# Weights in pieces, first loads in the order of use, last store by tiles: an RNN, LSTM, transformer block and expert layer in one kernel

## The reference

```python
x = x + rnn(x, cond)            # h = tanh(x_t Wx + b + h Wh), over 512 tokens
x = x + lstm(x, cond)           # four gates of 256, over 512 tokens
x = x + block(x, cond)          # hyperbolic attention (16 heads) and MLP, modulated by cond @ w_ada + b_ada
x = x + experts(x, cond)        # a shared MLP and the 2 best of 4 experts per sequence
```

## Time and profile before

| what | value |
|---|---|
| runs (3) | 2505.90, 2506.37, 2506.92 us |
| profiled execution, its own time | 2505.63 us |
| its span, first to last instruction | 2503.8 us |
| TensorE products busy | 2350.1 us (94%) |
| TensorE weight loads busy | 1574.1 us (63%) |
| VectorE busy | 1574.7 us (63%) |
| ScalarE busy | 1346.1 us (54%) |
| GpSimd busy | 566.6 us (23%) |
| moved by DMA | 102.71 MB, mean 41 GB/s |
| granted TensorE clock, mean | 0.985 |

### The profile page before, as it was taken

The page is one execution under the profiler, slowest core; times in us unless marked ns, Lnnn a source line. Parts: engine busy times, 40 slices in busy tenths (PEclk is TensorE's granted clock), DMA queues, the critical chain, the costliest instruction groups (busy, mean ns, idle before and its releaser), DMA issues.

```text
span 2503.8 us, 96005 instructions
## 1 busy us (share of the span) xinstructions
PE 2350.1 (94%) x39628; PEld 1574.1 (63%) x39628; DVE 1574.7 (63%) x7212; ACT 1346.1 (54%) x4508; POOL 566.6 (23%) x1176
## 2 busy tenths in 40 slices
PE   7899999999999999999757999999999999999999
PEld 5677777777777777777333664646656465564666
DVE  4777777777777877777456556645465464655330
ACT  3554555555555555555737556565565655556332
POOL 0222222232223222232221212212032221312100
PEclk9999999999999999999978999999999999999999
DMA  3111001000000001000103003030020301102020
GB/s 111 43 59 44 24 25 37 26 30 25 27 29 25 29 21 36 25 23 15 64 0 114 1 1 122 1 123 1 18 106 1 123 1 52 71 1 98 1 80 9
DMA packets 45382, 102.71 MB, mean 41 GB/s; under 512 B 9476, under 2 KB 26500, under 8 KB 40212
## 3 DMA queue, kind: packets, MB, share of 16 engines
q1 hardware_dynamic: 41684, 94.06, 10.8%
q10 hardware_dynamic: 3264, 2.52, 0.3%
HBM read 75.53 MB, written 21.04 MB: 39 GB/s over the span
## 4 chain that ended last, share of the span: by engine, by line
PE 45%; ACT 3%; issue 2%; DVE 1%; POOL 0%; DVEq 0%; ACTq 0%
PE bank L1203 13%; PE bank L1190 13%; PE bank L1369 4%; PE bank L1361 4%; PE bank L1284 3%; ACT pexp L1910 2%; PE bank L1269 2%; PE bank L1334 1%; PE bank L1254 1%; PE bank L1295 1%; PE bank L1220 1%; ACT dump L1848 0%; POOL S L1980 0%; DVE spl L1668 0%; PE bank L1380 0%
## 5 line engine op out<-in xcount | busy, mean ns | idle before, releaser
L135 PE MATMUL psFI<-wh,Hs 128*8 128x128 f32 (+3 forms) x8192 | 325.9, 277 | 60.2 <-DVE Hs L252 45.3
L135 PE MATMUL psOR<-wh,RH 128*16 128x128 f32 (+3 forms) x8320 | 322.6, 273 | 7.6 <-DMA Hs<-in_condP 2.9
L135 PEld LDWEIGHTS psFI<-wh,Hs 128*8 128x8 f32 (+3 forms) x8192 | 182.9, 99 | 177.8 <-DVE Hs L252 175.6
L1910 ACT ACTIVATE pexp<-bank 128x1024 f32<-128x1024 f32 x256 | 242.9, 1024 | 37.0 <-PE bank L1269 36.1
L336 ACT ACTIVATE RH<-RT 128x16 f32<-128x16 f32 x512 | 110.8, 216 | 260.7 <-DVE RT L256 260.7
L1203 PE MATMUL bank<-ew,hidden 128*128 128x256 f32 x1024 | 240.4, 381 | 0.0
L1190 PE MATMUL bank<-x3T,ew 128*128 128x512 f32 x512 | 239.2, 595 | 0.0
L1203 PEld LDWEIGHTS bank<-ew,hidden 128*128 128x128 f32 x1024 | 192.4, 190 | 69.3 <-issue 48.0
L327 ACT ACTIVATE sFI<-FIT 128x32 f32<-128x32 f32 x512 | 118.6, 232 | 204.4 <-DVE FIT L236 199.6
L236 DVE STREAM_TRANSPOSE FIT<-psFI 128x128 f32<-128x128 f32 x512 | 162.1, 317 | 104.9 <-PE psFI L135 102.0
L135 PEld LDWEIGHTS psOR<-wh,RH 128*16 128x16 f32 (+1 forms) x8320 | 206.3, 104 | 10.6 <-issue 6.2
(11 more groups left out here) (347 smaller groups left out, 4498.0 us busy)
## 6 DMA issues: line engine op xcount, KB each, us to landing
ew<-in_ew SPq DMA_DIRECT2D x32, 1024.0 KB, 9.1
qkv_scratch<-qkvr SPq DMA_DIRECT2D x31, 384.0 KB, 2.8
big<-qkv_scratch SPq DMA_DIRECT2D x7, 1536.0 KB, 7.8
XX<-in_xT SPq DMA_DIRECT2D x32, 256.0 KB, 2.7
x_scratch<-xr SPq DMA_DIRECT2D x32, 128.5 KB, 2.4
x<-x_scratch SPq DMA_DIRECT2D x8, 514.0 KB, 9.0
ada<-ada_scratch SPq DMA_DIRECT2D x8, 512.0 KB, 8.6
out_x<-x SPq DMA_DIRECT2D x8, 512.0 KB, 3.3
```

Source lines behind the costliest of these rows:

```text
L135: last = pe.matmul(bank[32 * j:32 * j + width, :], state(k), weights[:, k, j, cols], start=False, stop=k == KC - 1, tile_position=(0, 32 * ...
L1910: up(act.activation(M.pexp[:, n % 2, 2 * pr:2 * pr + 2, :], M.PS[pr][:, :, :], ACT.Exp, scale=1.0 / math.sqrt(HD)), "exps")
```

## The change

At the start, ScalarE's queue has the bias first, SyncE's has r, wx, x chunk 0 and then the two copies of h; TensorE waits for r and wh before slot 0 and for the copies of h only in slot 8. x chunks 1 and 2 leave after slots 9 and 12. w_ada is cut into six pieces of 256 KB, two each after slots 2, 5 and 8; wqkv and its bias are cut into nine pieces of 128 KB, three each after slots 15, 19 and 23; the waits for them move to where they are used. `Weights.pieces` cuts the large weights into 34 pieces of 128 KB, 256 columns of one block of rows each; with the small ones there are 42 entries. SyncE's loop issues three of them per chunk, at three places between its other transfers (two in chunk 1).

At the end, the third part (n = TOPK) of the last sequence's `down` adds into four banks, one a tile (`last_bank`). Its last two steps run tile by tile (`last_downs`), each tile raising the semaphore; the vector engine waits per tile, and SyncE stores each tile of 128 KB when it is ready.

```diff
@@ recurrences, tensor
-            pe.wait_ge(sem["ld_wh0"], 16)
-            pe.wait_ge(sem["ld_states"], 48)
+            pe.wait_ge(sem["ld_wh0"], 32)
...
-                    if n:
-                        pe.wait_ge(sem["hL"], n)
+                    pe.wait_ge(*((sem["hL"], n) if n else (sem["ld_states"], 32)))
@@ recurrences, scalar
+            act.dma_start(R.bias[:, :], A["bias"]).then_inc(sem["ld_bias"], 16)
             act.dma_start(R.wh[:, :, :, R_], A["wh"][:, :, :, R_]).then_inc(sem["ld_wh0"], 16)
-            act.dma_start(R.bias[:, :], A["bias"]).then_inc(sem["ld_bias"], 16)
@@ recurrences, sync
+            sp.dma_start(r_of(-1), A["condP"]).then_inc(sem["ld_wh0"], 16)
+            sp.dma_start(R.wx[:, :, :, R_], A["wx"][:, :, :, R_]).then_inc(sem["ld_wx0"], 16)
             sp.dma_start(R.XX[0][:, :, :], A["xT"][0]).then_inc(sem["x_in_0"], 16)
-            sp.dma_start(R.wx[:, :, :, R_], A["wx"][:, :, :, R_]).then_inc(sem["ld_wx0"], 16)
-            sp.dma_start(r_of(-1), A["condP"]).then_inc(sem["ld_states"], 16)
...
-            for c in (1, 2):
-                sp.dma_start(R.XX[c][:, :, :], A["xT"][c]).then_inc(sem[f"x_in_{c}"], 16)
             sp.wait_ge(sem["ld_lstm"], 32)
             F.loads(sp)
+            for j in range(3):
+                sp.wait_ge(sem["tR"], 3 * j + 3)
+                F.load_conditioning(sp, j)
+            for c in (1, 2):
+                sp.wait_ge(sem["tR"], 3 * c + 7)
+                sp.dma_start(R.XX[c][:, :, :], A["xT"][c]).then_inc(sem[f"x_in_{c}"], 16)
...
+                if k == 1:
+                    for n in range(3):
+                        sp.wait_ge(sem["tR"], CH + 4 * n)
+                        F.load_products(sp, n)
+                else:
+                    weight(1)
                 Q.load(sp, k - 4)
                 F.store_qkv(sp, k - 3)
+                weight(1)
                 F.store_x(sp, k - 1)
-                for dst, src in itertools.islice(loads, 1):
-                    sp.dma_start(dst, src).then_inc(W.loaded, 16)
+                weight(1)
@@ Weights
+    def pieces(dst, src, shape):
+        if len(shape) == 2 or shape[2] <= D:
+            rows = 1 if shape[-1] == D else shape[1]
+            return [(dst[:, k:k + rows], src[:, k:k + rows]) for k in range(0, shape[1], rows)]
+        return [(dst[:, k, c:c + D], src[:, k, c:c + D]) for k in range(shape[1]) for c in range(0, shape[2], D)]
@@ AttentionInputs
-        sp.dma_start(self.wada[:, :, :], A["w_ada"]).then_inc(self.wada_in, 16)
-        for dst, src in ((self.W.I[:, :], A["I"]), (self.wqkv[:, :, :], A["wqkv"]), (self.bqkv[:, :], A["bqkv"].partition_broadcast(P))):
-            sp.dma_start(dst, src).then_inc(self.wqkv_in, 16)
+        sp.dma_start(self.W.I[:, :], A["I"]).then_inc(self.wada_in, 16)
+    def load_conditioning(self, sp, j):
+        cols = slice(2 * j * D, 2 * (j + 1) * D)
+        for k in range(KC):
+            sp.dma_start(self.wada[:, k, cols], self.A["w_ada"][:, k, cols]).then_inc(self.wada_in, 16)
+    def load_products(self, sp, n):
+        cols = slice(n * D, (n + 1) * D)
+        for k in range(KC):
+            sp.dma_start(self.wqkv[:, k, cols], self.A["wqkv"][:, k, cols]).then_inc(self.wqkv_in, 16)
+        sp.dma_start(self.bqkv[:, cols], self.A["bqkv"][cols].partition_broadcast(P)).then_inc(self.wqkv_in, 16)
...
                 if i == 12:
-                    pe.wait_ge(self.wada_in, 16)
+                    pe.wait_ge(self.wada_in, 16 * (1 + 3 * KC))
...
                         if c == 0 and n == 0:
                             pe.wait_ge(self.ada_made, 3)
+                            pe.wait_ge(self.wqkv_in, 16 * 9)
@@ tensor_round
-        for q in range(NQ):
-            last = pe.matmul(M.y_bank(q), ..., start=m == 0 and q % 2 == 0, ...)
+        y_bank = M.last_bank if e == NB - 1 and n == TOPK else M.y_bank
+        for q in range(NQ):
+            last = pe.matmul(y_bank(q), ..., start=m == 0 and (y_bank == M.last_bank or q % 2 == 0), ...)
+    def last_downs():
+        for q in range(NQ):
+            for i in (STEPS - 2, STEPS - 1):
+                if q == 0:
+                    pe.wait_ge(*at("hidden", e, i + 1))
+                last = pe.matmul(M.last_bank(q), ..., start=False, stop=i == STEPS - 1, ...)
+            last.then_inc(M.sem("edown"), 1)
@@ vector_round
-        dve.wait_ge(*at("edown", e))
+        last = e == NB - 1
         for q in range(NQ):
+            if last or q == 0:
+                dve.wait_ge(*at("edown", e, STEPS - 1 + q if last else None))
@@ sync_round
+    if b == NB:
+        for q in range(NQ):
+            sp.wait_ge(*at("x3_out", e, q + 1))
+            sp.dma_start(out[e, q * P:(q + 1) * P, :], M.x3[:, q, :]).then_inc(M.sem("out"), 16)
+        sp.wait_ge(*at("out", e, 16 * NQ))
```

More of the change, by code:

```diff
@@ L364, in _, with weight @@
         def _(sp):
+            sp.dma_start(r_of(-1), A["condP"]).then_inc(sem["ld_wh0"], 16)
+            sp.dma_start(R.wx[:, :, :, R_], A["wx"][:, :, :, R_]).then_inc(sem["ld_wx0"], 16)
             sp.dma_start(R.XX[0][:, :, :], A["xT"][0]).then_inc(sem["x_in_0"], 16)
-            sp.dma_start(R.wx[:, :, :, R_], A["wx"][:, :, :, R_]).then_inc(sem["ld_wx0"], 16)
-            sp.dma_start(r_of(-1), A["condP"]).then_inc(sem["ld_states"], 16)
             sp.dma_start(h_of(LAG - 1), A["condP"]).then_inc(sem["ld_states"], 16)
             sp.dma_start(h_alone(LAG - 1), A["condP"]).then_inc(sem["ld_states"], 16)
-            for c in (1, 2):
-                sp.dma_start(R.XX[c][:, :, :], A["xT"][c]).then_inc(sem[f"x_in_{c}"], 16)
             sp.wait_ge(sem["ld_lstm"], 32)
             F.loads(sp)
+            for j in range(3):
[4 more added lines that the diff above has]
+                sp.dma_start(R.XX[c][:, :, :], A["xT"][c]).then_inc(sem[f"x_in_{c}"], 16)
             loads = iter(W.loads)
+            def weight(n):
+                for dst, src in itertools.islice(loads, n):
+                    sp.dma_start(dst, src).then_inc(W.loaded, 16)
             for k in range(1, NCH + 1):
@@ L406, in __init__ @@
             self.of[name] = sb("W_" + name, shape)
-            self.loads.append((self.of[name][tuple([slice(None)] * len(shape))], A[name]))
+            self.loads += self.pieces(self.of[name], A[name], shape)
         for name, width in (("bo", D), ("bf2", D), ("sb2", D)):
@@ L417, in __init__ @@
         self.ones, self.half, self.mhalf = sb("ones_", [P, P]), sb("half", [P, 3 * H]), sb("mhalf", [P, NQ])
+    @staticmethod
+    def pieces(dst, src, shape):
[3 more added lines that the diff above has]
+        return [(dst[:, k, c:c + D], src[:, k, c:c + D]) for k in range(shape[1]) for c in range(0, shape[2], D)]
 class AttentionInputs:
@@ L771, in slot @@
             if i == 27:
-                dve.wait_ge(self.wqkv_in, 48)
+                dve.wait_ge(self.wada_in, 16 * (1 + 3 * KC))
                 dve.tensor_copy(self.W.I16[:, :], self.W.I[:, :])
@@ L1163, in expert, with last_bank @@
         return (self.W["sw1"], self.W["sw2"], self.W["sb1"]) if n == 0 else (self.ew1[n - 1], self.ew2[n - 1], self.eb1[:, n - 1, :])
+    def last_bank(self, q):
+        return self.bank(q)[:, 0:D]
     def y_bank(self, q):
@@ L1201, in down @@
             pe.wait_ge(*at("y_act", e, n * NQ))
+        y_bank = M.last_bank if e == NB - 1 and n == TOPK else M.y_bank
         for q in range(NQ):
-            last = pe.matmul(M.y_bank(q), M.hidden[:, i % HIDDEN, q * P:(q + 1) * P], M.expert(n)[1][:, m, :],
-                             start=m == 0 and q % 2 == 0, stop=m == FC - 1, skip_group_check=True)
+            last = pe.matmul(y_bank(q), M.hidden[:, i % HIDDEN, q * P:(q + 1) * P], M.expert(n)[1][:, m, :],
+                             start=m == 0 and (y_bank == M.last_bank or q % 2 == 0), stop=m == FC - 1, skip_group_check=True)
         last.then_inc(M.sem("edown"), 1)
+    def last_downs():
[3 more added lines that the diff above has]
+                    pe.wait_ge(*at("hidden", e, i + 1))
+                last = pe.matmul(M.last_bank(q), M.hidden[:, i % HIDDEN, q * P:(q + 1) * P], M.expert(TOPK)[1][:, i % FC, :], start=False, stop=i == STEPS - 1, skip_group_check=True)
+            last.then_inc(M.sem("edown"), 1)
     def steps(lo, hi):
@@ L1350, in tensor_round @@
         steps(5, STEPS)
-        for i in range(IN_NEXT, STEPS):
+        for i in range(IN_NEXT, STEPS - 2):
             down(i)
+        last_downs()
     if front:
@@ L1490, in last_outputs @@
         dve.wait_ge(*at("y", e))
-        dve.wait_ge(*at("edown", e))
+        last = e == NB - 1
         for q in range(NQ):
-            up(dve.scalar_tensor_tensor(M.x3[:, q, :], M.y_bank(q), M.wm[:, 1, q:q + 1], M.x3[:, q, :], ALU.mult, ALU.add), "x3_out")
+            if last or q == 0:
+                dve.wait_ge(*at("edown", e, STEPS - 1 + q if last else None))
```

(7 more changed lines are left out.)

1 line of the change is left out of this document (removed).

## The result

The changed kernel takes 2493.48 us (median of 6 runs, 2492.56 to 2494.30), the kernel before in the same sessions 2507.05 us (2505.90 to 2509.30): a ratio of 0.9945, 95% interval 0.9935 to 0.9955, 13.6 us less. 2493.0 was forecast. The profiled execution took 2493.44 us with a span of 2491.7; the span of before was 2503.8, so the profile has 12.1 us of it.

A forecast was written before the change was run, and what follows sets the result against it. TensorE, busy 94%, bounds the kernel, losing time at the start, in stops behind large loads, and at the end. Terms -3.3 - 3.5 - 5.4 + 0.5 - 1.7 = -13.4 from 2505.6, plus 0.7 for the median: 2493.0 us, range 2490 to 2498.

The forecast's parts named there:

- (a): Start: first loads in order of use let slot 0 start at about 7.6 instead of 10.93; -3.3 us.
- (b): Early slots: w_ada, wqkv and bias in pieces no longer hold up the instruction packet; -3.5 us, added waits 0.
- (c): Scan: the large weights in 128 KB pieces remove the stops behind the four 1 MB loads; -5.4 us.
- new cost: Pieces right behind other transfers at some 40 places, and perhaps a delayed first instruction packet; +0.5 us.
- (d): End: last store by tiles, issued 1.18 us earlier, with 128 KB landing 0.3 to 0.7 us sooner; -1.7 us.
- The last will land at about the same time, 7.0: Step under (a): slot 0's needed loads, from the same two queues, finish about when they did before.
- rival 2: Start gives half, through first x behind wx and copy, or first instruction packet behind wh: -1.3, 2495 us; chance 0.10.
- The early bias: Start, under (a): if the earlier bias helps, slot 0 starts at 7.2, the good bound of -3.7 us.
- Rival 3: Scan stops are not the loads' doing; (b), (c) and the +0.5 go, leaving -5.0: 2501.4 us; chance 0.04.
- the packet waited for one DMA's share and not for the queue: Step under (b): an instruction packet waits for one DMA's share per engine; 16 KB keep it 1.1 us at most.
- rival 1: Instruction packet waits for all queued data, so early w_ada and wqkv pieces act like 1 MB loads: 2496 us; chance 0.14.
- Rival 4: Chunk loads: each piece behind another SP transfer makes its own stop, 40 in 14 chunks: 2509 us; chance 0.02.

The follow-up runs named there:

- second profile: The changed kernel itself, unchanged, run and profiled again in four more runs: 2494.08 us, ratio 0.9951 to the kernel before.
- e10_x_act: Changed kernel with x chunk 0 moved to ScalarE's queue, between the bias and wh: 2492.66 us (4 runs), ratio 0.9949 to the kernel before.
- e1_whole: Changed kernel with the four large weights whole again, one 1 MB DMA per chunk in chunks 2 to 5, behind the x store: 2501.01 us.
- e5_wada_whole: Changed kernel with w_ada as one 1.5 MB DMA again, right behind the small loads: 2496.59 us.
- e9_quarters: Changed kernel with each large weight as four 256 KB DMAs issued back to back, one weight per chunk in chunks 2 to 5: 2497.34 us.
- e2_burst: Changed kernel with all eight 128 KB pieces of one large weight issued back to back behind the x store, in chunks 2 to 5: 2493.24 us.
- e3_runs: Changed kernel with each large weight as one 1 MB DMA again, but in runs of 1 KB: 2498.51 us.
- e6_wada_burst: Changed kernel with all pieces of w_ada, wqkv and its bias issued back to back behind the small loads, without waits for slots: 2497.05 us.

## Why the prediction was right

By its own terms, from the profiles of before and of the change:

| term | forecast | bounds given | measured | how |
|---|---|---|---|---|
| (a) start | -3.3 | -3.7 to -2.1 | -2.3 | tanh of slot 7, 20.54 to 18.23; -1.5 in the second profile |
| (b) w_ada in pieces | -3.5 | -3.7 to -1.5 | -3.4 | slots 7 to 10, 10.34 to 6.91 |
| (c) large weights in pieces | -5.4 | -5.4 to -4.0 | -5.2 | slots 10 to 95, 198.48 to 193.27 |
| new cost | +0.5 | 0 to +2 | +1.2 | slots 95 to 511 +0.7, from there to the last product +0.6 |
| (d) end | -1.7 | -1.9 to -1.0 | -2.4 | last product to end of span, 5.1 to 2.7 |
| sum | -13.4 | | -12.1 | spans |

The time was met to 0.5 us, but that is luck: in the profiles the sum is 1.3 us short of the forecast (10.7 against 13.4, 2.7 short, with the second profile of the change), and errors of +1.0, +0.7 and -0.7 in (a), the new cost and (d) partly cancel in it; the medians differ by 13.6.

(a) had the right mechanism, one state copy in place of three, and the wrong size; the second profile, with -1.5, is outside its bounds. "The last will land at about the same time, 7.0" was the step: x landed at 8.2, 1.1 us after wx, because as the last in SyncE's queue it shared the engines with the LSTM's 1 MB loads (e10_x_act, with x ahead of them, starts slot 0 at 7.50). That is what rival 2 named, the first x behind wx and the copy, with half the gain gone; it came due in large part, 1.0 us in one profile and 1.8 in the other of the 2.0 it priced. The early bias helped nothing: x ended the wait. The LSTM's weights landed at 13.3 (2.52 + 10.8), as foreseen, and slot 5 did not wait.

(b) and (c) held in size: with the 1 MB and 1.5 MB loads gone the stops are gone, and e1_whole and e5_wada_whole bring each back by itself. Rival 3 is out, also by the count of instructions under e1_whole: every stop begins at the same number of instructions past the packets that had come. The prediction said that no run shows TensorE's store of instructions; this count shows its end, as TensorE never gets more than 449 products and weight loads beyond 256 for each packet. But the step under (b), "the packet waited for one DMA's share and not for the queue", is wrong; rival 1's mechanism, with 0.14, was nearer, though a packet does not wait for all that has been issued either. e9_quarters and e2_burst show more than one DMA to count, and e3_runs shows that the number of runs does not. The row that I built on, wqkv landing after the instruction packet, may be explained without it: wqkv was issued 0.9 us after w_ada, and the packet then due may have come before it reached the engines; this is not shown. Rival 1's price (+3) did not come due: with the change all four first pieces of w_ada had been issued by 17.2 us, but the packet came at 18.36, right behind the landing of the first (18.28) and before that of the second (18.98). 0.43 us of the price is in the second profile. That the pieces of the large weights are spread is not what saves them either (e2_burst, with packets up to 1.7 us late but no stop): it is that they are small against the time of an issue.

Rival 4's fear was for small pieces behind other transfers, 40 of them. There is hardly a trace of it: from slot 95 to slot 511 the change takes 946.13 us, e2_burst 946.08 and e1_whole, which cuts none of the later stage's weights, 946.07, against 945.46 in the one profile of before. What these 0.6 us are was not found; the pieces they are not. But a piece behind an x store can stop TensorE now and then: 0.32 us in e6_wada_burst, whose loads in that stretch are those of the change, one place of some 40.

The other part of the new cost lies behind the scan, where the code is unchanged until the very end. From the tanh of slot 511 to the last product it is 1323.9 us before, 1324.5 with the change and 1322.7 to 1325.3 over the twelve others. Where these two differ by 0.5 us, at the change from scan to rounds, the rows by stretch of before and after are:

```profile
1210.00:1216.00 6.00, 2.28 (x20) 1.06 (x20) 4.09 (x10) 4.38 (x8) 0.86 (x1) 0.83 0.07 30
```

```profile
1200.00:1206.00 6.00, 2.84 (x20) 1.79 (x20) 3.89 (x9) 4.23 (x8) 0.79 (x1) 0.57 0.03 12
```

The granted clock is 0.83 in the one and 0.57 in the other, over the same 20 products. When TensorE, half idle in this stretch, is at 1.2 and when at 2.4 GHz differs from run to run, and that is worth a microsecond or so either way: 10 us earlier, from 1200 to 1205, TensorE was busy throughout in before at a granted clock of 0.66 and started 26 products; in e2_burst, in the same stretch (1191.05 to 1196.05), it had 1.00 and started 42. What sets the moment is not shown. The 1.5 us that I added to the low end for this were of the right size.

(d) was outside its bounds, by 0.5: the landing of 128 KB was taken from the x store of the scan (2.6 us), and at the end it takes 1.7. Beside the scan's stores other loads ran, at the end nothing runs but the tile before; that this is the reason was not tested.

## What to carry to other kernels

A large DMA can cost an engine that doesn't wait for it: look for "issue" idle time in the middle of a run of products, and for the instruction queue's packet that comes some 2.4 us before it ends. Where TensorE starts some 60 products and weight loads a microsecond, keep what is queued at any time to 128 KB or little more (two DMAs, 256 KB in all, still stopped it now and then): cut the loads, and send the pieces no faster than the engines move them; for pieces of 128 KB the place in the chunk did not matter. What the first products need goes ahead of the first large load in every queue, not only in its own, and the last store is small.

## What the runs showed of the hardware that was not expected

- TensorE stops for want of instructions at a fixed count: all 25 stops, in eight of the fourteen profiles, begin 449 products and weight loads beyond 256 for each packet (numbered from 0, the first in the trace), and end 2.3 to 2.6 us after the next packet.
- The instruction packet comes late behind data in another queue, also when that is in several DMAs (four of 256 KB, 0.47 us apart: stops of 0.34 to 0.99 us) and also when it is in runs of 1 KB (1 MB: 0.39 to 1.27 us). How much of a queue it waits for was not measured.
- The length of the stops at one place varies: behind the first 1 MB load 0.61 us in the kernel before and 2.52 in e1_whole.
- A 256 KB load in runs of 256 B, issued at 1.2 to 1.5 us, lands between 6.1 and 9.6 us, by what else is queued; a 256 KB load in runs of 2 KB, first in its queue or behind the bias alone, at 3.5 to 4.5.
- The start alone varies by 0.7 us between executions of kernels with the same first loads (slot 0 at 8.67 to 9.39).
- At the end, where little else is moved, a store of 128 KB lands 1.7 us after its issue, one of 512 KB 2.9; in the scan one of 128.5 KB took 2.6.
